# First feed-forward stage of a gated cross-attention block as seven block products per weight tile, in two passes over the tokens

## What is computed

```python
x = x + tanh(g_xattn[0]) * xattn(layernorm(x), ctx_2048, Wq, Wk, Wv)   # 32 heads of 32, 750 keys
x = x + tanh(g_ffn[0]) * ffn(layernorm(x), w1, w2, w3)

def _quantize(w):
    gamma = jnp.mean(jnp.abs(w))
    return jnp.clip(jnp.round(w / (gamma + EPS)), -1.0, 1.0)
def _bitlinear(x, w):
    return jnp.matmul(x, _quantize(w).T)
x1 = _bitlinear(x, w1); x2 = _bitlinear(x, w2)     # 1024 -> 2816
hidden = jax.nn.sigmoid(x1) * x2
return _bitlinear(hidden, w3)                      # 2816 -> 1024
```

## Time and profile before

| | us |
|---|---|
| median of three executions (lowest, highest) | 2431.76 (2431.45, 2432.7) |
| the profiled execution | 2427.1 |
| its span, first to last instruction | 2425.3 |
| PE busy | 2369.5 |
| DVE busy | 1433.3 |
| ACT busy | 1348.3 |
| POOL busy | 854.1 |

### The profile page before, as it was taken

How to read it: one execution, slowest core, us unless ns; L and a number is a source line. 1 busy time by engine, 2 the same in 40 slices (tenths; PEclk the granted TensorE clock), 3 DMA queues, 4 the chain that set the end, 5 groups by cost and what they waited for, 6 DMA issues and landing times.

```text
span 2425.3 us, 48902 instructions
## 1 busy us (share of the span) xinstructions
PE 2369.5 (98%) x18386; PEld 1405.3 (58%) x18386; DVE 1433.3 (59%) x2537; ACT 1348.3 (56%) x2894; POOL 854.1 (35%) x857
## 2 busy tenths in 40 slices
PE   7999999999999999999999999989999999999999
PEld 5885565666666666666666666555555555544444
DVE  6666676786777777777777867664444444410000
ACT  5876787787787787887877877752111111110000
POOL 3664254564645545555545646430000000000000
PEclk9999999999999999999999999999999999999999
DMA  7785434434334443433434333453333333244351
GB/s 254 237 257 177 126 105 111 119 96 113 109 94 128 108 115 96 113 116 84 134 103 117 92 87 107 110 178 122 110 99 108 100 107 98 83 139 136 111 165 52
DMA packets 250123, 298.10 MB, mean 123 GB/s; under 512 B 110624, under 2 KB 205344, under 8 KB 249376
## 3 DMA queue, kind: packets, MB, share of 16 engines
q1 hardware_dynamic: 249888, 294.98, 41.6%
HBM read 196.22 MB, written 49.55 MB: 101 GB/s over the span
## 4 chain that ended last, share of the span: by engine, by line
PE 32%; POOL 28%; issue 28%; DMA 1%; DVE 1%; ACT 1%; POOLq 1%; SPq 0%; DVEq 0%; ACTq 0%
PE ps L1453 20%; POOL krs L705 14%; PE ps L1578 11%; POOL oinv L723 4%; POOL kms L700 3%; POOL osum L721 2%; POOL osum L728 2%; POOL ca L735 2%; POOL cn L749 1%; POOL oinv L725 1%; DMA hid<-hidden 1%; POOLq L60 0%; POOL crs L745 0%; DMA wraw<-in_wffn 0%; ACT pf L953 0%
## 5 line engine op out<-in xcount | busy, mean ns | idle before, releaser
L1485 PE MATMUL ps<-wk,cpair 128*128 128x512 f16 x4608 | 1116.8, 379 | 5.1 <-DVE cpair L1081 4.6
L1278 DVE TENSOR_TENSOR plo<-pf,phi 125x448 f16<-125x448 f32 x768 | 504.7, 658 | 203.0 <-ACT phi L944 196.7
L1485 PEld LDWEIGHTS ps<-wk,cpair 128*128 128x128 f16 x4608 | 398.8, 97 | 378.2 <-DVE cpair L1081 5.7
L953 ACT ACTIVATE pf<-ps 125x448 f32<-125x448 f32 x768 | 416.9, 543 | 244.9 <-PE ps L1505 232.8
L1453 PE MATMUL ps<-xnTh,w12q 128*128 128x512 f16 (+1 forms) x1408 | 477.6, 353 | 2.9 <-issue 2.1
L1453 PE MATMUL ps<-xnTl,w12q 128*128 128x512 f16 (+1 forms) x1408 | 477.5, 353 | 0.0
L944 ACT ACTIVATE phi<-pf 125x448 f16<-125x448 f32 x768 | 444.4, 579 | 8.5
L705 POOL TENSOR_TENSOR krs<-kms,mhalf 125x8 f32<-125x8 f32 x192 | 328.6, 1712 | 15.0
L1505 PEld LDWEIGHTS ps<-qT,kst 128*125 128x125 f16 x1536 | 208.1, 137 | 148.9 <-DMA kst<-kpair 4.2
L1529 PE MATMUL ps<-val,phi 125*128 125x65 f16 x3072 | 279.0, 192 | 12.0 <-DVE plo L1278 11.8
L700 POOL TENSOR_TENSOR kms<-kss,keps 125x8 f32<-125x8 f32 x192 | 72.3, 376 | 616.5 <-DVE kss L1233 616.5
(11 more groups left out here) (115 smaller groups left out, 2653.2 us busy)
## 6 DMA issues: line engine op xcount, KB each, us to landing
gbuf<-in_wffn SPq DMA_DIRECT2D x66, 512.0 KB, 4.8
wraw<-in_wffn SPq DMA_DIRECT2D x66, 512.0 KB, 5.7
kst<-kpair SPq DMA_DIRECT2D x128, 250.0 KB, 4.6
cstream<-in_ctx SPq DMA_DIRECT2D x48, 500.0 KB, 4.3
craw<-in_ctx SPq DMA_DIRECT2D x48, 500.0 KB, 5.6
hid<-hidden SPq DMA_DIRECT2D x7, 2816.0 KB, 12.7
hidden<-hh SPq DMA_DIRECT2D x66, 256.0 KB, 2.1
kst<-kpair SPq DMA_DIRECT2D x128, 125.0 KB, 2.5
```

The costliest lines, as they stand in the source:

```text
L953: act.activation(pf[0:KW, e % 6, :], bank(3 + e % 3)[0:KW, 0:2 * S], ACT.Exp, bias=LN128, scale=SCALE).then_inc(p_ready, 1)
L1278: dve.tensor_tensor(plo[0:KW, e % 6, :, :], pf[0:KW, e % 6, :].rearrange("p (t n) -> p t n", t=2), phi[0:KW, e % 6, :, :], ALU.subtract).t ...
L1485: mm = pe.matmul(bank(pt)[:, :], cpair[:, n % RING, a, kc, :], wkp[g][:, w, kc, :], start=(kc == 0 and m == 0), stop=(kc == KC - 1 and m = ...
```

## The change

Stage C is written anew. The product of a stacked weight matrix (w1, w2) and the normalised x is split into 2 by 2 blocks: w1 and w2 by the two halves of K, and x by the halves of K and by the two halves (112 tokens) of each batch. Each tile j then takes seven block products in place of eight, by Winograd's form of Strassen's scheme. A pass takes the tokens of four batches, 448 columns per block; there are two passes of 22 **superpieces**, n = 0 to 43. In a superpiece the seven products P1, P5, P7, P6, P2, P3, P4 are made in this order, each of 8 matmuls of 448 columns; P2, P3 and P4 are added onto P1, P5 and P7 in their banks after ACT has copied those out (`keep_product`).

- **POOL** makes the four weight combinations T1, T3, T2, T4 of each superpiece (`combos`, 512 columns of bfloat16 each), and two sums of products (s57 and c22, 448 columns).
- **DVE** makes three sums of products (u2, c12, c21), two products with the sigmoids (into hf) and two low halves; in the first pass it quantises w1 and w2 for the next superpiece, in the second one tile of w3 per superpiece.
- **SP** saves each pair of quantised w1 and w2 to DRAM in the first pass (`save_w12`) and loads it in the second (`load_w12`); hidden is stored in pieces of 112 tokens, four DMAs per superpiece.
- **The combinations of x**: after normalisation POOL adds and subtracts halves of a batch (`ln_combine`, four instructions of 512 columns per batch), and the low halves become four instructions per batch (one of them half as wide) in place of two, at new times. 28 of 56 half tiles are transposed at the end of B, the others two per superpiece in superpieces 3 to 16, between products. The last batch's norm runs in superpieces 0 to 7 (`LATE_STATS`, `LATE_NORM`, `LATE_LOW`).
- Stage B pads the queries' high and low halves to 240 columns, the buffer of weights for the means is one instead of two, and stage A frees a buffer earlier. Stage D is the same.

```diff
-CH = ((0, 512), (512, 512), (1024, 512), (1536, 256))
+BLK = 7
+HD = D // 2
+CW = TOK // 4
+NSP = 2 * FJ
...
-    cn_d = nc.dram_tensor("x1_normalised", [TOK, 2, D], F16, kind="Internal").ap()
+    cn_d = nc.dram_tensor("x1_blocks", [B, 4, LT, 2, D], F16, kind="Internal").ap()
+    w12_d = nc.dram_tensor("w12_ternary", [FJ, P, 2, D], BF16, kind="Internal").ap()
...
-        LN_STAGES = {"stats": (4, 5), "rstd": (5, KT), "norm": (KT, KT + 1), "high": (KT, KT + 2),
-                     "low": (KT + 1, KT + 3)}
-
-        def ln_tiles(u, t, stage):
-
-            return [2 * b + h for b in range(B) for h in range(2)
-                    if (G * b + G + 1) * KT + LN_STAGES[stage][h] == u * KT + t]
+        LN_STATS, LN_RSTD, LN_NORM = (4, 5), (5, 6), (6, 7)
+        LN_HIGH, LN_LOW = (6, 9, 11, 13), (7, 10, 12, 14)
+        LN_COMB = (8, 10)
...
+        NX = BLK * (B // 2)
...
+        X_FIRST = 3
+        LATE_STATS, LATE_NORM, LATE_LOW = (0, 1), (2, 3), (4, 5, 6, 7)
+
+        def late_halves(n):
+
+            h = NX + 2 * (n - X_FIRST)
+            return (h, h + 1) if NX <= h < 2 * NX else None
...
+            def cn_save(ld):
+                w = pair_width(ld % 4)
+                sp.wait_ge(cnl_ready, ld + 1)
+                sp.dma_start(cn_d[ld // 4, ld % 4, :, :, 0:w], cn[0:LT, :, 0:w]).then_inc(cn_saved, 16)
...
+            def save_w12(j):
+                sp.wait_ge(wquant_ready, 2 * j + 2)
+                sp.dma_start(w12_d[j, :, :, :], w12q[:, j % 2, :, :, :].rearrange("p m k n -> p m (k n)")
+                             ).then_inc(w12_saved[j % 2], 16)
...
+            for n in range(FJ):
+                if n:
+                    for half in range(2):
+                        save_hid(n - 1, half)
+                if n in LATE_LOW:
+                    cn_save(4 * B - 4 + LATE_LOW.index(n))
+                if late_halves(n + 2):
+                    while next_stage < 4 * B and halves_in(next_stage) <= late_halves(n + 2)[1] + 2:
+                        load_stage(next_stage)
+                        next_stage += 1
+                if n + 1 < FJ:
+                    save_w12(n + 1)
+                if n + 2 < FJ:
+                    load_w(n + 2)
...
+            def ln_low(b, q):
+                w = pair_width(q)
+                pool.wait_ge(cnh_ready, 4 * b + q + 1)
+                pool.tensor_tensor(cn[0:LT, 1, 0:w], block_pair(b, q), cn[0:LT, 0, 0:w], ALU.subtract
                                    ).then_inc(cnl_ready, 1)
+
+            def ln_combine(b, n):
+
+                e, o = ca[0:LT, 2 * b % 4, :], ca[0:LT, (2 * b + 1) % 4, :]
+                lo, hi = slice(0, HD), slice(HD, D)
+                pool.wait_ge(cn_ready, 2 * b + 2)
+                pool.wait_ge(cnl_ready, 4 * b + n + 1)
+                if n == 0:
+                    pool.tensor_tensor(e[:, lo], e[:, lo], o[:, lo], ALU.subtract).then_inc(comb_ready, 1)
+                    pool.wait_ge(comb_ready, 4 * b + 1)
+                    pool.tensor_tensor(o[:, lo], o[:, lo], o[:, hi], ALU.add).then_inc(comb_ready, 1)
+                else:
+                    pool.tensor_tensor(o[:, hi], o[:, hi], e[:, lo], ALU.subtract).then_inc(comb_ready, 1)
+                    pool.wait_ge(comb_ready, 4 * b + 3)
+                    pool.tensor_tensor(e[:, hi], e[:, hi], o[:, hi], ALU.subtract).then_inc(comb_ready, 1)
+
+            def combos(n):
+
+                w, t = w12q[:, n % 2, :, :, :], wT[:, n % 2, :, :, :]
+                if n < FJ:
+                    pool.wait_ge(wquant_ready, 2 * n + 2)
+                else:
+                    pool.wait_ge(w12_in[n % 2], 16 * ((n - FJ) // 2 + 1))
+                if n >= 2:
+                    pool.wait_ge(h_ready, product(n - 2, P4))
+                w11, w21, w12, w22 = w[:, 0, 0:4, :], w[:, 0, 4:8, :], w[:, 1, 0:4, :], w[:, 1, 4:8, :]
+                pool.tensor_tensor(t[:, 0, :, :], w12, w11, ALU.subtract).then_inc(t_ready, 1)
+                pool.tensor_tensor(t[:, 1, :, :], w22, w12, ALU.subtract).then_inc(t_ready, 1)
+                pool.wait_ge(t_ready, combo(n, T1))
+                pool.tensor_tensor(t[:, 2, :, :], w22, t[:, 0, :, :], ALU.subtract).then_inc(t_ready, 1)
+                pool.wait_ge(t_ready, combo(n, T2))
+                pool.tensor_tensor(t[:, 3, :, :], w21, t[:, 2, :, :], ALU.subtract).then_inc(t_ready, 1)
 
...
+            def superpiece(n):
+
+                pool.wait_ge(prod_copied, 3 * n + 3)
+                wait(pool, c22_ready, n)
+                pool.tensor_tensor(s57[:, :], prod[:, n % 2, 1, :], prod[:, n % 2, 2, :], ALU.add).then_inc(s57_ready, 1)
+                pool.wait_ge(u2_ready, n + 1)
+                pool.wait_ge(s57_ready, n + 1)
+                wait(pool, hf_ready, 2 * n)
+                pool.tensor_tensor(c22[:, :], u2[:, n % 2, :], s57[:, :], ALU.add).then_inc(c22_ready, 1)
+                if n + 1 < NSP:
+                    combos(n + 1)
+
+            for n in range(NSP):
+                superpiece(n)
+                if n in LATE_STATS:
+                    ln_rstd(NL - 2 + LATE_STATS.index(n))
+                if n in LATE_LOW:
+                    q = LATE_LOW.index(n)
+                    ln_low(B - 1, q)
+                    if q < 2:
+                        ln_combine(B - 1, q)
...
+                keep_product(n, 0)
+                if n:
+                    hidden_high(n - 1, 1)
+                keep_product(n, 1)
+                keep_product(n, 2)
+                if late_halves(n):
+                    x_out(late_halves(n)[0], other + 3)
+                gate(n, 0)
+                if late_halves(n):
+                    x_out(late_halves(n)[1], other)
+                hidden_high(n, 0)
+                gate(n, 1)
+                if n in LATE_LOW:
+                    ln_high(B - 1, LATE_LOW.index(n))
...
+            def ternary(dst, src, m, done):
+
+                count = sum(quantised.values())
+                wait(dve, wquant_ready, quantised["w12"])
+                wait(dve, w3_ready, quantised["w3"])
+                dve.tensor_scalar(wneg[:, :], src, thr[:, 2, m:m + 1], None, ALU.is_lt).then_inc(wneg_ready, 1)
+                dve.wait_ge(wneg_ready, count + 1)
+                dve.scalar_tensor_tensor(out=dst, in0=src, scalar=thr[:, 1, m:m + 1], in1=wneg[:, :],
+                                         op0=ALU.is_gt, op1=ALU.subtract).then_inc(done, 1)
...
+            def quantise(j, m):
+
+                s = j % 2
+                if m == 0:
+                    dve.wait_ge(w_in[s], 32 * (j // 2 + 1))
+                    wait(dve, w12_saved[s], 16 * (j // 2))
+                    if j >= 2:
+                        dve.wait_ge(h_ready, product(j - 2, P4))
+                        dve.wait_ge(t_ready, combo(j - 2, T4))
+                ternary(w12q[:, s, m, :, :].rearrange("p k n -> p (k n)"), wraw[s][:, m, :], m, wquant_ready)
+                quantised["w12"] += 1
+
...
+            for n in range(NSP):
+                b0 = 4 * (n % 2)
+                if n:
+                    hidden_low(n - 1, 1)
+                next_weights(n, 0)
+                dve.wait_ge(h_ready, product(n, P6))
+                dve.wait_ge(prod_copied, 3 * n + 1)
+                if n >= 2:
+                    dve.wait_ge(c22_ready, n - 1)
+                dve.tensor_tensor(u2[:, n % 2, :], bank(b0 + 3)[:, 0:CW], prod[:, n % 2, 0, :], ALU.add
+                                  ).then_inc(u2_ready, 1)
+                next_weights(n, 1)
+                dve.wait_ge(h_ready, product(n, P3))
+                dve.wait_ge(u2_ready, n + 1)
+                wait(dve, hl_ready, 2 * n - 1)
+                dve.tensor_tensor(hf[:, 0, :], bank(b0 + 1)[:, 0:CW], u2[:, n % 2, :], ALU.add).then_inc(c12_ready, 1)
+                dve.wait_ge(sg_ready, 2 * n + 1)
+                dve.wait_ge(c12_ready, n + 1)
+                dve.tensor_tensor(hf[:, 0, :], hf[:, 0, :], sg[:, 0, :], ALU.mult).then_inc(hf_ready, 1)
+                dve.wait_ge(h_ready, product(n, P4))
+                wait(dve, sg_ready, 2 * n)
+                dve.tensor_tensor(c21[:, :], bank(b0 + 2)[:, 0:CW], u2[:, n % 2, :], ALU.add).then_inc(c21_ready, 1)
+                hidden_low(n, 0)
+                dve.wait_ge(sg_ready, 2 * n + 2)
+                dve.wait_ge(c22_ready, n + 1)
+                wait(dve, hl_ready, 2 * n)
+                dve.tensor_tensor(hf[:, 1, :], c22[:, :], sg[:, 1, :], ALU.mult).then_inc(hf_ready, 1)
+                if n in LATE_STATS:
+                    ln_stats(NL - 2 + LATE_STATS.index(n))
+                if n in LATE_NORM:
+                    ln_norm(NL - 2 + LATE_NORM.index(n))
+            hidden_low(NSP - 1, 1)
...
+            def block_product(n, bk, blk, weights, first):
+
+                x = xT[n // FJ]
+                for kc in range(4):
+                    for part in range(2):
+                        mm = pe.matmul(bank(4 * (n % 2) + bk)[:, 0:CW], weights[:, kc, :], x[:, part, blk, kc, :],
```

(41 more changed lines are left out.)

504 lines of the change are left out of this document (247 added, 257 removed).

## The result

| | before | after |
|---|---|---|
| median (lowest, highest), us | 2432.23 (2431.45, 2432.76) | 2530.15 (2528.39, 2533.71) |
| span of the profiled execution | 2425.3 | 2526.6 |
| stage B | 1406.7 | 1483.7 |
| stage C, first and second pass | 544.1 | 326.3 + 243.3 |
| stage D | 270.5 | 270.3 |

What follows compares the result with a forecast made beforehand. PE's matmul columns were taken to bound stages B, C and D. 2427.1 - 2 (C) + 16 + 1 (B) - 1 (D) = 2441 us, with 4.7 for the median 2446 us; range 2404 to 2482.

Steps and rivals of the forecast that it cites:

- PE sets C before; 10.6 us per superpiece after: Stage C: PE's matmul columns set the time before; afterwards 10.6 us per superpiece, 11.5 in superpieces 3 to 16.
- Exclusion of DVE and POOL, 11.5 to 12 us: Stage C, first pass: DVE and POOL exclude each other, 13.4 us of work less overlaps, 11.5 to 12 per superpiece.
- POOL's 1.19 us for 512 columns of bfloat16: POOL's combining instructions: 1.19 us for 512 columns, from the straight line; bfloat16 itself had no row.
- Rival 3: Stage C: POOL becomes the bound at 1.5 us per combination, total 2485 us, deciding from about 1.3; chance 0.10.
- The weight loop, 12.3: Stage C, first pass: save, weight loads, landing and DVE's quantisation close once per superpiece, 12.3 us per turn.
- The long loop, 4 x 21.1: Superpieces 4 to 7: the last batch's low-half store goes ahead of save and loads, 21.1 us each, four times.
- The pass change, 14: Stage C: the second pass's first superpiece takes 14 us, its reload being issued behind two w3 loads.
- C in all: Stage C: 305 us for the first pass and 237 for the second, 542 together against 544.1 before.
- Stage B, g = 2: 2.3 us x 7 = 16: Stage B: POOL's low half and two combinations delay krs, costing PE 2.3 us in seven units, 16 us.
- the rest of the norm's work is hidden by POOL's idle half of B: Stage B: remaining norm work, one-buffered weight means, pads' memsets and later context load cost 0 to 3 us, taken as 1.
- The clock at no cost: Long loop of stage C: PE idles about 9 us per superpiece, and whatever clock it loses falls in idle time.
- Stage D, 1 us less: Stage D: unchanged except that its first 1.5 us of waiting goes; 1 us less in the sum.

Runs made afterwards that it cites:

- run 6: POOL's four weight combinations per superpiece shrunk from 512 to 8 columns, PE multiplying plain w1 and w2 blocks instead, against the kernel of run 4: 2459.22 us.
- run 4: First-pass weight loads of superpiece n + 2 issued at the head of superpiece n's block, ahead of the stores and save, against the changed kernel: 2493.81 us.
- run 8: DVE instead of POOL makes the four weight combinations in the first pass, against the kernel of run 4: 2485.71 us.
- run 11: Kernel of run 9 with DVE making the first pass's weight combinations and also s57 and c22: 2397.61 us, ratio to before 0.9854.
- run 5: Changed kernel with later low halves and second combinations, weight loads first, w12 reload ahead of w3 loads, hidden's first load at the second pass's end: 2422.21 us.
- run 1: Store of low half q = 2 put ahead of the keys' second stacking in each batch's last unit, against the changed kernel: 2490.62 us.
- run 2: Low half q = 1, second combinations, and high and low halves q = 2 and 3 one tile later, against the changed kernel: 2473.37 us.
- run 9: Store of the last batch's low half moved behind the hidden stores of the next superpiece's block, against the kernel of run 5: 2417.52 us.

## Why the prediction was wrong in size

Slower was the likelier side and the forecast, but at 2446 us; measured were 2530, outside 2404 to 2482. By its steps:

- **PE sets C before; 10.6 us per superpiece after.** Right: the second pass goes at 10.6, and superpieces with transposes at 11.4 where nothing else holds them (11.5 forecast; run 6).
- **Exclusion of DVE and POOL, 11.5 to 12 us.** Right in kind, 12.2 in run 4; what POOL hinders was somewhat undercounted. Runs 6, 8 and 11 show it. The page SBUF — State Buffer of the Trainium skill (section Who interferes with whom) gives this exclusion; by its rule the trace agrees, at 2.03 against 1.28 us for one instruction.
- **POOL's 1.19 us for 512 columns of bfloat16.** Right by the straight line: 1.15 unhindered. Rival 3 had its point of decision at 1.3; with the hindered 1.54 POOL is still not what PE waits for in the second pass.
- **The weight loop, 12.3.** Right, 12.5 to 13.8, 12.7 in the mean. Its parts in the turn shown: 6.8 and 5.7 us, against 6.6 and 5.7 in the sum (12.3).
- **The long loop, 4 x 21.1.** Right in mechanism and count, 4 x 23.4 measured (93.7 us), 9 us short. The part that was too small is the one in the queue: 10.4 us from the store's issue to wneg against 7.3 in the sum. From the save to wneg alone pass 9.0 to 9.6 us in these turns, 7.2 in the settled ones; why the loads land later there was not tried. DVE and POOL took 13.5 of the 13.8 forecast (the rest of the 23.95). Its superpieces were PE's 5 to 8, not 6 to 9.
- **The pass change, 14.** Measured 17.9 + 11.9 for 12.3 + 14 forecast, 3.5 us more. The reload stood behind two w3 loads, and its wait showed one superpiece earlier.
- **Not in the sum: the load of hidden's first block.** 2.8 MB are issued at 2043.85, early in the second pass, ahead of a w12 reload: 7.6 us. With the edit of run 5 they are gone. The load stood in the kernel; it was counted as loaded early for D and not as traffic in the way of others.
- **C in all:** 569.6 for 542 forecast.
- **Stage B, g = 2: 2.3 us x 7 = 16.** Right in size, 2.6 x 7, and in what delays khat. But PE waits for khat itself, ahead of the next tile's projections (L1698, 7 waits, 17.0 us), and not for the plo behind it: before, khat ended 0.8 us ahead of these projections, where the sum took 1.4 us of slack from plo. khat came 3.3 us later in the unit, 3.7 in the sum. The two misses partly cancel, so the size owes something to luck.
- **Stage B, "the rest of the norm's work is hidden by POOL's idle half of B", 0 to 3 us. This is the step that failed.** Stage B as a whole lost 77 us for 17 in the sum. About 57 of the 84 us missed are the seven g = 3 units, some 8 us each. The step asked whether POOL had time. It did not ask who waits for the one cn buffer, which is now written four times per batch in place of twice, nor what stands ahead of its store in SP's queue. Both were in the change. Runs 1 and 2 show it: another place in the queue gives 39.5 us back, and one tile more of time 56.8 (the khat wait included). The other 18 to 21 us stay in both runs; their cause is open.
- **The clock at no cost** was assumed for C, as falling into idle time; no run tests that. In B it does not fall there: the stretches above show 0.58 and 0.54 just when PE had work. How much of the 57 us it is was not separated.
- **Stage D, 1 us less** was forecast; it gave 0.2.

Most of what B and C lost was a matter of order and times: mending these alone gives 108 to 113 us (runs 5 and 9), and the kernel is then 12 to 15 us below the one before. With POOL's first-pass work moved to DVE as well (run 11) the seven products pay 35 us, and not the 67 of their columns: stage C takes 493.1 us, 51.0 less than before, since the first pass stays at DVE's pace with 11.4 us and the late norm's superpieces keep 12.7 to 15, and stage B still takes 19.0 us more than before.

## What to carry to other kernels

For every buffer that a change writes more often, follow one full round (producer, the store's place in its queue and what that queue waits for ahead of it, the landing, the next writer), and price it as a wait of the next writer's whole engine. A store that waits for a late producer goes behind everything that is ready; a load goes ahead. Where two engines exclude each other, add up their work and not only each one's own: here 13.4 us less the overlaps came out at 12.2 per superpiece. Moving instructions onto the busier one was then a gain, as it took 0.42 and 0.62 us for what the other took 1.15 and 1.13 for.

## What was not expected of the hardware

- POOL's rate for 512 columns is the same in bfloat16 (1.15 us) as the float32 line gives (1.19); DVE's is not (0.42 against 0.69).
- After PE gaps of 2.4 and 3.1 us the granted clock fell to the 1.2 GHz level not in the gap, but 1.3 and 0.4 us into the work behind it, for some 3 us each time (0.81, then 0.58, and 0.54 in the rows above). Not every such gap does it: behind the one of 2.4 us before 501.67 in the changed kernel the clock stays at 1.00 for the next 9 us. In run 2's g = 3 unit (675 to 720 us), where no gap of PE is longer than 1.0 us, the granted clock is 1.00 throughout.
